# Rotating buffers for N, a split spread over the slots, and five loads issued from ScalarE

## What is computed

```
z = layernorm(ctx)                                  # 64 context rows a batch
q = layernorm(x) * ln2_w + ln2_b, then @ Wq         # 16 heads of 64
k, v = split((z * ln1_w + ln1_b) @ Wkv)
q = q * (1 + fside) + fside                         # per batch and head
x = x + softmax(q k^T / 8) v @ Wout
x = x + tanh(layernorm(x) @ weight @ aux1 @ aux2 + bias)
```

## Time and profile before

| | us |
|---|---|
| median of 3 runs | 2093.94 (2093.3 to 2094.66) |
| the profiled execution | 2092.8 |
| its span in the trace | 2091.0 |
| busy: TensorE | 2023.3 (97%) |
| busy: VectorE, ScalarE, GpSimd | 1562.4, 1364.9, 1359.5 |

### The profile page before, as it was taken

The page is one execution under the profiler, slowest core; times in us unless marked ns, Lnnn a source line. Parts: engine busy times, 40 slices in busy tenths (PEclk is TensorE's granted clock), DMA queues, the critical chain, the costliest instruction groups (busy, mean ns, idle before and its releaser), DMA issues.

```text
span 2091.0 us, 31989 instructions
## 1 busy us (share of the span) xinstructions
PE 2023.3 (97%) x9072; PEld 1665.0 (80%) x9072; DVE 1562.4 (75%) x2488; ACT 1364.9 (65%) x3125; POOL 1359.5 (65%) x1511
## 2 busy tenths in 40 slices
PE   8999999999899999999999999999999999999998
PEld 6877878888788787878877787878878787878877
DVE  7567876776677777777777777777777777777776
ACT  4456666666667666676666666766666666666655
POOL 2136767667566776667766676767666677667664
PEclk9999999999999999999999999999999999999999
DMA  7657989999788888988889788988778676777653
GB/s 257 197 176 218 274 228 254 261 247 262 211 234 248 218 233 218 260 222 228 217 233 255 213 233 221 247 232 223 217 215 224 200 211 189 223 210 199 181 169 123
DMA packets 529184, 464.12 MB, mean 222 GB/s; under 512 B 61040, under 2 KB 420592, under 8 KB 529008
## 3 DMA queue, kind: packets, MB, share of 16 engines
q1 hardware_dynamic: 529008, 462.07, 79.9%
HBM read 279.64 MB, written 182.26 MB: 221 GB/s over the span
## 4 chain that ended last, share of the span: by engine, by line
PE 48%; DVE 12%; POOL 11%; SPq 10%; issue 7%; DMA 6%; ACT 5%; DVEq 0%; ACTq 0%; POOLq 0%
PE bank L168 18%; PE bank L1221 12%; PE bank L173 9%; PE bank L1224 6%; POOL area L1510 5%; SPq L715 3%; DVE N_lo L766 3%; POOL area L1517 2%; DMA wo<-wo_scratch 2%; DVE pT_lo L1398 2%; POOL M_lo L999 2%; DMA m_scratch<-evac 2%; DVE area L1367 2%; DVE turned L1389 1%; SPq L713 1%
## 5 line engine op out<-in xcount | busy, mean ns | idle before, releaser
L1510 POOL TENSOR_TENSOR area<-area,row_max 128x256 f32<-128x256 f32 x512 | 353.4, 711 | 97.8 <-DVE row_max L1372 93.9
L1269 ACT CAST pT_hi<-turned 128x512 fp32r<-128x512 f32 x256 | 159.1, 621 | 390.5 <-DVE turned L1389 390.3
L168 PE MATMUL bank<-M_hi,xT_hi 128*128 128x512 f32 x1024 | 400.9, 391 | 11.8 <-ACT xT_hi L1058 11.8
L1221 PE MATMUL bank<-N_hi,pT_hi 128*128 128x512 f32 x1024 | 401.4, 392 | 3.9 <-ACT pT_hi L1269 2.6
L1221 PE MATMUL bank<-N_lo,pT_hi 128*128 128x512 f32 x1024 | 401.2, 392 | 0.0
L168 PE MATMUL bank<-M_lo,xT_hi 128*128 128x512 f32 x1024 | 400.8, 391 | 0.0
L1534 POOL TENSOR_TENSOR area<-area 128x512 f32<-128x512 f32 x127 | 165.2, 1301 | 300.5 <-ACT area L1310 300.5
L1517 POOL TENSOR_TENSOR area<-area,row_inv 128x512 f32<-128x512 f32 x256 | 268.6, 1049 | 113.9 <-DVE row_inv L1381 113.9
L1378 DVE TENSOR_REDUCE row_sum<-area 128x8 f32<-128x512 f32 x256 | 174.4, 681 | 167.5 <-ACT area L1264 166.6
L173 PE MATMUL bank<-M_hi,xT_lo 128*128 128x512 f32 x1024 | 275.9, 392 | 4.0 <-POOL xT_lo L1063 4.0
L1398 DVE TENSOR_TENSOR pT_lo<-turned,pT_hi 128x512 fp32r<-128x512 f32 x256 | 194.6, 760 | 111.5 <-ACT pT_hi L1269 110.0
(11 more groups left out here) (190 smaller groups left out, 3984.7 us busy)
## 6 DMA issues: line engine op xcount, KB each, us to landing
p_scratch<-area SPq DMA_DIRECT2D x256, 256.0 KB, 2.7
p_moved<-p_scratch SPq DMA_DIRECT2D x512, 128.0 KB, 4.6
area<-x_dram SPq DMA_DIRECT2D x128, 256.0 KB, 5.2
area<-x_turned_dram SPq DMA_DIRECT2D x128, 256.0 KB, 4.4
x_scratch<-area SPq DMA_DIRECT2D x127, 256.0 KB, 3.1
x_moved<-x_scratch SPq DMA_DIRECT2D x508, 64.0 KB, 4.1
y_dram<-area SPq DMA_DIRECT2D x127, 256.0 KB, 4.1
land<-m_scratch SPq DMA_DIRECT2D x120, 256.0 KB, 3.8
```

Of the source, the lines that this page charges most:

```text
L168: mm = eng.matmul(ps, sh, mv, start=(n == 0), stop=False)
L1221: pe.matmul(O_ps[:], st(pT_hi, k), n_cols(mv, k), start=(k == 0 and mv is N_hi), stop=False)
L1269: act.copy(half_of(pT_hi, q), turned[:]).then_inc(s_pTh[q], 1)
L1510: last = pool.tensor_tensor(s, s, row.to_broadcast([P, 2, 4, J2]), ALU.subtract)
```

## The change

Four buffers, N_hi, N_lo, Wo_hi and Wo_lo, become one rotating set. A stacked pair's result is staged in the two that are free, each block is split with hi into another buffer and lo in place, and `n_stage` is gone. Only an even batch b is split at its border, slot 8b + 1 (`border`): ScalarE's copies in two groups of four, five of VectorE's subtractions there, and three of the blocks' lo parts (`BY_POOL`) by GpSimd. ScalarE may start when TensorE has done the hi and lo passes of that slot's O (`s_nfree`). The odd batch b0 + 1 is split one block a slot over the even batch's slots (`split_at`: slots 34 to 41 for batch 5, and so on), one copy by ScalarE and one subtraction by VectorE, after `pT_hi` and `pT_lo` of half 0. The V load becomes three transfers whose destination has 128 rows and whose source names the same 64 rows twice. All five loads of a pair are issued from ScalarE: `load_v2` for the next slot's pair between exp(0) and the layernorm statistics, `load_wo2` after ScalarE's copies of the bank. For the first pair of each kind (slot 25) all five are issued at the slot's end. `store_wo` moves one slot earlier. Some semaphores of the last tile are merged with those of the others. The core of the diff:

```diff
+        with nc.sbuf_tensor("n_raw", [P, 4 * PAIRS * D], F32) as n_raw:
+            pass
         N_hi, N_lo = sb("N_hi", PAIRS * D, F32R), sb("N_lo", PAIRS * D, F32R)
-        with nc.sbuf_tensor("n_stage", [P, 2 * PAIRS * D], F32) as n_stage:
-            pass
...
+        n_bufs = (N_hi, N_lo, Wo_hi, Wo_lo)
+        n_at = {b: (0, 1) for b in range(STACKED)}
+        used, free = 1, (2, 3)
+        for b0 in range(STACKED, B, 2):
+            n_at[b0], n_at[b0 + 1] = (used, free[0]), (0, free[1])
+            used, free = free[1], (used, free[0])
+        N_of = lambda b: [n_bufs[i] for i in n_at[b]]
+        stage_of = lambda b, c: n_raw[:, (n_at[b][1] * PAIRS + c) * D:(n_at[b][1] * PAIRS + c + 1) * D]
+        BY_POOL = (4, 5, 6)
+        BY_DVE = {0: [c for c in range(PAIRS) if c not in BY_POOL], 1: list(range(PAIRS))}
+        split_at = {TPB * b + c - TPB + 2: (b, c) for b in range(STACKED + 1, B, 2) for c in range(PAIRS)}
+        border = lambda t: t % TPB == 1 and t // TPB in range(STACKED, B, 2)
...
-            for half in range(2):
-                dst = v2_raw[half * DH:(half + 1) * DH, :]
-                sp.dma_start(dst[:, 0:P].rearrange("e (b j) -> e b j", b=2), even[:, b0:b0 + 2, :]).then_inc(s_vin, 16)
-                for i in range(2):
-                    sp.dma_start(dst[:, P + i * CTX:P + (i + 1) * CTX], odd[:, b0 + 1 - i, :]).then_inc(s_vin, 16)
+            twice = lambda a: a.unsqueeze(0).to_broadcast([2, *a.shape])
+            eng.dma_start(v2_raw[:, 0:P].rearrange("p (b j) -> p b j", b=2), twice(even[:, b0:b0 + 2, :])).then_inc(s_vin, 16)
+            for i in range(2):
+                eng.dma_start(v2_raw[:, P + i * CTX:P + (i + 1) * CTX], twice(odd[:, b0 + 1 - i, :])).then_inc(s_vin, 16)
...
@@ slot_sp
-            if t + 1 in stacked_at:
-                load_v2(sp, *stacked_at[t + 1])
-            if 10 <= t < 26:
-                store_wo(sp, t - 10)
+            if 9 <= t < 25:
+                store_wo(sp, t - 9)
...
-            if t + 1 in stacked_at:
-                load_wo2(sp, *stacked_at[t + 1])
@@ slot_pe
+                    if border(t):
+                        mm.then_inc(s_nfree, 1)
@@ slot_act
             elif t > 2:
+                if t + 1 in stacked_at and not first_stacked(t + 1):
+                    load_v2(act, *stacked_at[t + 1])
                 if t + 1 < T:
                     ln1_stats(act, t + 1, (t + 1) % RING)
...
+            if t + 1 in stacked_at and not first_stacked(t + 1):
+                load_wo2(act, *stacked_at[t + 1])
             evacuate("C")
+            if border(t):
+                n2_hi(act, t // TPB, range(0, 4))
             if tile_of(t - 1):
                 pT_hi_part(0, t - 1)
+            if border(t):
+                n2_hi(act, t // TPB, range(4, 8))
+            if t in split_at:
+                b, c = split_at[t]
+                n2_hi(act, b, [c])
...
-            elif m == 1 and TPB * STACKED < t < T:
-                n2_hi(act, t // TPB)
+            if first_stacked(t + 1):
+                load_v2(act, *stacked_at[t + 1])
+                load_wo2(act, *stacked_at[t + 1])
@@ slot_dve
                 turn_p(0, t - 1)
+                if border(t):
+                    n2_lo(dve, t // TPB, BY_DVE[0][0:2])
...
                 pT_lo_part(0, t - 1)
+            if border(t):
+                n2_lo(dve, t // TPB, BY_DVE[0][2:])
+            if t in split_at:
+                b, c = split_at[t]
+                n2_lo(dve, b, [c])
...
-            elif m == 1 and TPB * STACKED < t < T:
-                n2_lo(dve, t // TPB)
@@ slot_pool
+            if border(t):
+                n2_lo(pool, t // TPB, BY_POOL)
```

More of the change, by code:

```diff
@@ L605, in build @@
         s_x2a, s_x2n = sem("s_x2a"), sem("s_x2n")
-        s_fl, s_fbl, s_thl, s_last = (sem(n) for n in ("s_fl", "s_fbl", "s_thl", "s_last"))
+        s_last, s_nfree, s_nl_pool = sem("s_last"), sem("s_nfree"), sem("s_nl_pool")
         s_yl, s_bnl, s_rsl = sem("s_yl"), sem("s_bnl"), sem("s_rsl")
@@ L690, in build @@
         nth_pair = lambda b0, p: PAIRS * (b0 - STACKED) // 2 + p
-        stage_of = lambda b, c: n_stage[:, (b % 2 * PAIRS + c) * D:(b % 2 * PAIRS + c + 1) * D]
+        n_bufs = (N_hi, N_lo, Wo_hi, Wo_lo)
[8 more added lines that the diff above has]
+        BY_DVE = {0: [c for c in range(PAIRS) if c not in BY_POOL], 1: list(range(PAIRS))}
+        lo_before = lambda b: PAIRS * min(b, STACKED) + sum(len(BY_DVE[a % 2]) for a in range(STACKED, b))
+        split_at = {TPB * b + c - TPB + 2: (b, c) for b in range(STACKED + 1, B, 2) for c in range(PAIRS)}
+        first_stacked = lambda t: t == TPB * (STACKED - 1) + 2
+        border = lambda t: t % TPB == 1 and t // TPB in range(STACKED, B, 2)
         n2_ps = banks[2:4]
@@ L750, in n2_evacuate @@
             eng.wait_ge(s_n, n_tiles(n, h) + 1)
-            eng.wait_ge(s_nl, PAIRS * (b0 - 1) + p + 1)
+            eng.wait_ge(s_o, TPB * (b0 - 1))
             if n == 0:
@@ L755, in n2_evacuate, with n2_hi, n2_lo, n2_made @@
             copy(stage_of(b0 + 1 - h, p)[DH:P], n2_ps[h][DH:P, :]).then_inc(s_nev, 1)
-        def n2_hi(act, b):
-            act.wait_ge(s_o, TPB * b)
-            for c in range(PAIRS):
-                act.wait_ge(s_nev, 2 * nth_pair(b - b % 2, c) + 2)
[L761 to L765, removed]
-                dve.tensor_tensor(n_cols(N_lo, c), stage_of(b, c), n_cols(N_hi, c).bitcast(F32), ALU.subtract).then_inc(s_nl, 1)
+        def n2_hi(act, b, cs):
+            for c in cs:
+                if b % 2:
+                    act.wait_ge(s_o, TPB * (b - 1))
+                else:
+                    act.wait_ge(s_nfree, b - STACKED + c // 4 + 1)
+                act.wait_ge(s_nev, 2 * nth_pair(b - b % 2, c) + 2)
+                act.copy(n_cols(N_of(b)[0], c), stage_of(b, c)).then_inc(s_nh, 1)
+        def n2_lo(eng, b, cs):
+            for c in cs:
+                eng.wait_ge(s_nh, PAIRS * b + c + 1)
+                hi, lo = (n_cols(y, c) for y in N_of(b))
+                eng.tensor_tensor(lo, stage_of(b, c), hi.bitcast(F32),
+                                  ALU.subtract).then_inc(s_nl if c in BY_DVE[b % 2] else s_nl_pool, 1)
+        def n2_made(pe, b, q):
+            of_half = range(4 * q, 4 * q + 4)
+            pe.wait_ge(s_nl, lo_before(b) + sum(c < 4 * q + 4 for c in BY_DVE[b % 2]))
+            if b % 2 == 0 and any(c in BY_POOL for c in of_half):
+                pe.wait_ge(s_nl_pool, len(BY_POOL) * ((b - STACKED) // 2) + sum(c < 4 * q + 4 for c in BY_POOL))
         m_where = lambda c: ((c // 2) % 4, 2 * (c // 8) + c % 2)
@@ L1214, in slot_pe @@
                 if tile_of(t - 2):
-                    if m == 2:
+                    if m == 2 and u < TPB * STACKED:
                         pe.wait_ge(s_nl, u + 4 + 4 * q)
+                    elif m == 2:
+                        n2_made(pe, u // TPB, q)
+                    hi, lo = N_of(u // TPB)
                     ks = range(4 * q, 4 * q + 4)
@@ L1219, in slot_pe @@
                     for k in ks:
-                        for mv in (N_hi, N_lo):
-                            pe.matmul(O_ps[:], st(pT_hi, k), n_cols(mv, k), start=(k == 0 and mv is N_hi), stop=False)
+                        for mv in (hi, lo):
+                            mm = pe.matmul(O_ps[:], st(pT_hi, k), n_cols(mv, k), start=(k == 0 and mv is hi), stop=False)
+                    if border(t):
+                        mm.then_inc(s_nfree, 1)
                     pe.wait_ge(s_pTl[q], u + 1)
                     for k in ks:
-                        mm = pe.matmul(O_ps[:], st(pT_lo, k), n_cols(N_hi, k), start=False, stop=(k == 7))
+                        mm = pe.matmul(O_ps[:], st(pT_lo, k), n_cols(hi, k), start=False, stop=(k == 7))
                     if q == 1:
```

30 lines of the change are left out of this document (15 added, 15 removed).

## The result

The changed kernel takes 2130.3 us, median of four runs (2123.91 to 2130.95), against 2093.62 of the kernel before: a ratio of 1.0171, 95% interval 1.0149 to 1.0193. It is 36.7 us slower, where 10 were forecast. The profiled execution is the run of 2123.91 us. The busy times by stretch, to set against the earlier trace rows: slots 26 to 33; 34 and 35 (the first even border's loss falls in them); 42; 45; 100 to 105.

A forecast was written before the change was run, and what follows sets the result against it. TensorE, busy 97%, was taken as the bound, with a nearly as long loop of other engines behind it. Stalls of 12.4 + 47x, 70.2 us at x = 1.23 in place of 59.5, added 10.7 to 2092.8: 2104 us, range 2056 to 2142.

The forecast's parts named there:

- The likeliest case: Slot-to-slot loop of the other engines, lengthened by V's issues, outlasts TensorE's slot: 2104 us, range 2090 to 2140, chance 0.60.
- 12.4 + 47x: Predicted TensorE stalls in us over slots 26 to 121: loop excess less bank plus first pair, with 47 V loads.
- x: Loop time added per V load by three ScalarE issues between exp(0) and statistics: 1.23 us taken, 0 to 2.0 considered.
- the fast rival: ScalarE's V issues hardly reach exp(1): x = 0 gives 2046 us, x = 0.5 gives 2069; chance 0.24.
- the forecast's 70.2 us of stalls: TensorE's stalls predicted with x = 1.23, in place of 59.5 us in the kernel before.
- The second rival: V's transfers run on two DMA engines, costing 1.3 us in each of 28 early stacked slots: 2140 us, chance 0.10.
- Even borders.: VectorE's five subtractions make the border slot's loop 17.16 us; GpSimd's three are covered; TensorE's later xT_hi wait goes.
- the first pair's: V of the first pair, issued at slot 25's end and wanted early, was estimated to add 1.5 us of stalls.
- Splits.: VectorE's one-a-slot subtraction for odd borders lengthens the unstacked loop from 13.50 to 14.18 us for 48 slots.
- The bank.: How far the loop may fall behind before TensorE waits: 2.7 us, read at V's low part, subtracted once.
- SyncE's and ScalarE's wo2.: SyncE loses 4.5 us of issues a stacked slot, ending wo2 waits; wo2's issues on ScalarE fall in idle time, costing nothing.
- Signatures.: Signs in stacked slots: VectorE's exp(1) wait 1.45 to 2.7 us, slots 43 to 48 at 15.8; odd-border peaks gone.

The follow-up runs named there:

- V in six on ScalarE: Changed kernel with V loaded in six transfers of 64 rows instead of three, still issued by ScalarE between exp(0) and the statistics: 2206.6 us, ratio 1.0526.
- the change with the border on VectorE: Changed kernel with all eight low-part subtractions of an even border on VectorE, none on GpSimd: 2125.28 us, ratio 1.0150 to the kernel before.
- V in six on SyncE: Changed kernel with V in six 64-row transfers issued by SyncE: 2085.4 us with wo2 on SyncE, 2068.5 us with wo2 on ScalarE.

## Why the forecast was right or wrong

**Right: direction, place and mechanism.** The likeliest case, a loop of the other engines lengthened by V's issues between exp(0) and the statistics, is what happened. Its formula for the stalls, 12.4 + 47x, met three versions once x was measured:

| version | x | 12.4 + 47x | stalls counted |
|---|---|---|---|
| the change | 1.66 | 90.4 | 90.6 |
| V in six on ScalarE | 3.43 | 173.6 | 171.6 |
| wo2 back on SyncE | 2.56 | 132.8 | 135.0 |

It missed a fourth by 5.5 us. In the change with the border on VectorE x is 1.82 (start to start from the trace, mean of 47), the formula gives 97.9 and 92.4 were counted: the border's gain is not in it. The formula holds only where the loop is the longer side: at x = 0 it gives 12.4, while 29 to 47 us were counted with V in six on SyncE. No version came to the fast rival's 2046 us.

**Wrong: the size of x.** The prediction took an issue of 0.55 us, three alike, x = 1.23, with 2.0 as the upper end "if each issue meets one of SyncE's". The first two were 0.52 and 0.53, as taken; the third was 1.03 on average and up to 3.1. The step failed in treating the issue as a price of its own. It depends on the transfers ahead of it: on 64 rows the median stayed at 0.60 to 0.62 us in every place tried, with the twice-named source the last took 0.94 to 1.96 with the place and the load of the DMA engines. 47 x 0.43 = 20.2 us, which is the whole distance from the forecast's 70.2 us of stalls to 90.6, within 0.2. So the forecast's own sum, with x = 1.66, gives 2123.7 us for the profiled execution of 2123.9. The other 6 us to the median of 2130.3 lie between runs of the same kernel, and no trace shows them.

**The second rival was half right.** It saw that V's transfers run on few engines, but put the cost in DMA engines' time over a slot. There it was not: the DMA share was 0.88 in slots 26 to 33, as in the earlier trace rows, and 0.80 in slot 45. The cost was in the issuing queue. Both belong to one mechanism, and kept apart they were priced at 1.23 us and at 10 in 100.

**Two terms were off and cancelled.** *Even borders.* GpSimd's three subtractions were judged covered; the only risk named was to GpSimd's next work. What they did was to slow VectorE's from 0.68 to 1.76 us. The prediction had also said that TensorE's later wait for xT_hi goes; behind the six even borders that wait rose from 9.9 to 12.9 us. At x = 1.66 the prediction's terms give 78.6 us for stacked slots and borders, and 87.9 were counted, 9.3 more. Of these, 3.9 are the first pair's: slot 26 lost 5.4 us, where 1.5 was estimated. The rule that would have warned is the one named above, and the kernel before had a hint: pT_lo at 0.96 instead of 0.69 us, with GpSimd's subtraction for xT_lo beside it. *Splits.* 14.18 us a slot were forecast, 13.82 counted in slots 100 to 105: 2.3 us in the unstacked slots instead of 11.8. The subtraction is 0.68 us as taken, but two waits of VectorE further on shrank for it, by 0.54 us together. Before:

```profile
1719.47 0.75 DVE L1438 SCALAR_TENSOR_TENSOR area<-bank,rs,ffn_bias_row 128x512 f32<-128x512 f32 x1 [0.31 <-POOL rs L1522]
...
1723.45 0.78 DVE L1418 TENSOR_TENSOR x2T_lo<-turned,x2T_hi 128x512 fp32r<-128x512 f32 x1 [0.46 <-ACT x2T_hi L1290]
```

and after, with the split ahead of them:

```profile
1744.27 0.68 DVE L782 TENSOR_TENSOR Wo_hi<-n_raw,N_hi 128x512 fp32r<-128x512 f32 x1
...
1745.50 0.74 DVE L1474 SCALAR_TENSOR_TENSOR area<-bank,rs,ffn_bias_row 128x512 f32<-128x512 f32 x1
...
1749.48 1.00 DVE L1454 TENSOR_TENSOR x2T_lo<-turned,x2T_hi 128x512 fp32r<-128x512 f32 x1 [0.23 <-ACT x2T_hi L1314]
```

I had added the 0.68 to the loop without looking for idle time inside it.

**The bank.** The loop's lead was read at V's low part, 2.7 us. TensorE in fact waits for xT_lo (29.5 us in 43 waits). The lead is filled again in each unstacked stretch and used in each run, not once; that this and the other errors left the constant at 12.4 is luck.

**SyncE's and ScalarE's wo2.** wo2's waits went, as said (18.1 us before). The profile still puts one of 3.7 us down to wo2; it is the first pair's, and it ends 0.10 us after GpSimd has V's low part. wo2's issues cost nothing where they now stand. That moving it gained 40.6 us, by emptying the burst ahead of V's transfers, I had not seen.

**Signatures.** VectorE's wait for exp(1) rose from 166.6 us in 121 waits to 247.3 in 123, 1.7 us a V load where 1.25 was forecast; slots 43 to 48 last 16.3 us instead of 15.8; the odd borders' peaks are gone.

**Open.** With GpSimd's part in place, the even borders lose 34 to 37 us in all in the change and in the five versions whose stacked slots lose over 20 us behind slot 26, and 24 to 28 us in the four where these lose at most 16. V in six on ScalarE is in the first group (34.5), so the narrow transfers are not the cause by themselves. Most of the difference is TensorE's wait at L1243 for the border's low parts: 6.8 to 8.1 us in the first group, at most 2.0 in the second. That the other engines come to the border there without a lead would fit, but no run tested it. The first pair loses 5.4 us in slot 26 in the changed kernel and 6.0 in the kernel before; no run took that apart. Nor did one tell whether the block is held by the number of transfers outstanding or by their pieces. It does not last until a transfer has landed: in the changed kernel the third issue is over 1.0 to 2.5 us before the first landing.

## What to carry to other kernels

An issue is not a fixed price: put the queue's own rows for every transfer on the path, and ask what the queue does when the transfers ahead of it are narrow or the DMA engines are full. Fewer transfers can be a loss if each is spread over fewer DMA engines: with wo2 on ScalarE, V in three took 32 us more than V in six (by the ratios 28), though with all loads on SyncE the two were equal. Six issues of 0.6 us on a queue that waits anyway beat three on one that does not. Before giving part of a series of instructions to a second engine, check that the two do not slow each other, and look for idle time inside a loop before adding to it.

## What the runs showed of the hardware

- Of three back-to-back transfers whose source has an outermost dimension of 2, the first two issue in 0.5 to 0.8 us on average and the third holds its queue for 0.9 to 2.0, up to 3.5. On SyncE's queue and on ScalarE's alike. The next issue behind them is held in its turn (wo2's first: 2.21 us instead of 0.39). Issues onto 64 rows took 0.60 to 0.62 us (medians), six in a row, and single ones up to 2.25.
- Such a transfer leaves three semaphore updates, one onto 64 rows 16. The last of three such lands 3.4 us after the last issue, the last of six onto 64 rows 1.8 us (V on SyncE, wo2 on ScalarE).
- The hold is longer where the DMA engines have more to do: 1.07 us for two issues at a DMA share of 0.45, 3.22 at 1.17. This is a comparison of loads; no run changed the share alone.
- A float32 subtraction of 128 x 512 out of SBUF takes VectorE 0.68 us alone and 1.76 us beside the same on GpSimd, which takes 1.73 there and 1.35 at its shortest.
